# h's rows packed into 120: experts, shared adapter, logits, constant

## The reference, cut to what matters

```
# conditioning of x
q_emb = relu(cond @ W3 + b3)                         # 64 x 512
v     = (64 * x + sum_over_tokens(x)) * q_emb        # per batch
y     = relu(v @ W2 + b2)
# feed-forward with E = 6 routed adapters of rank R = 16, and one shared
base   = y @ W_base + b_base
shared = (y @ A_s) @ B_s
gates  = softmax(y @ W_router + b_router);  w = the two largest gates, 0 elsewhere
h      = y @ A_r[e] for each e;  routed = sum_e (h_e * w_e) @ B_r[e]
out    = x + base + shared + routed
```

## Time and profile before

| | us |
|---|---|
| median of 3 runs (lowest, highest) | 247.85 (246.45, 248.17) |
| the profiled execution | 246.59 |
| its span, first to last instruction | 244.9 |
| TensorE busy in it | 235.0 (96%) |
| DVE, ACT, POOL busy | 177.4, 102.1, 55.7 |

### The profile page before, as it was taken

The page is one execution under the profiler, slowest core; times in us unless marked ns, Lnnn a source line. Parts: engine busy times, 40 slices in busy tenths (PEclk is TensorE's granted clock), DMA queues, the critical chain, the costliest instruction groups (busy, mean ns, idle before and its releaser), DMA issues.

```text
span 244.9 us, 3159 instructions
## 1 busy us (share of the span) xinstructions
PE 235.0 (96%) x1007; PEld 189.4 (77%) x1007; DVE 177.4 (72%) x324; ACT 102.1 (42%) x206; POOL 55.7 (23%) x58
## 2 busy tenths in 40 slices
PE   7699599999999999999999999999999999999994
PEld 2577378888887878888888888888888888888883
DVE  0697898869988996679766995679756995351344
ACT  2247557234434445245533455145433455134330
POOL 5078971202312041012302121012202121000000
PEclk9769979999999999999999999999999999999999
DMA  7989990818016368019610567018000530013004
GB/s 151 299 198 208 270 249 1 170 69 280 0 58 116 146 200 171 0 43 299 143 33 0 183 197 137 0 43 300 0 0 0 192 150 0 0 53 120 3 0 173
DMA packets 32219, 28.49 MB, mean 116 GB/s; under 512 B 6173, under 2 KB 22621, under 8 KB 32206
## 3 DMA queue, kind: packets, MB, share of 16 engines
q1 hardware_dynamic: 32050, 28.33, 42.9%
q10 hardware_dynamic: 156, 0.00, 0.0%
HBM read 19.94 MB, written 8.39 MB: 116 GB/s over the span
## 4 chain that ended last, share of the span: by engine, by line
PE 69%; DVE 16%; SPq 6%; DMA 4%; issue 2%; POOL 1%; ACT 1%; POOLq 0%; DVEq 0%
PE m_ps L661 61%; PE hT L661 7%; DMA x_quart<-in_x_dram 4%; DVE xT L424 4%; DVE out_nat L548 3%; DVE x_sum L438 3%; SPq L217 2%; DVE vsum L429 2%; DVE y_lo L452 2%; SPq L205 1%; POOL x_full L284 1%; DVE x_lo L446 1%; SPq L211 1%; PE hT L748 1%; ACT x_hi L321 1%
## 5 line engine op out<-in xcount | busy, mean ns | idle before, releaser
L284 POOL TENSOR_TENSOR x_full<-x_sum,qT 128x512 f32<-128x512 f32 x31 | 37.9, 1222 | 138.5 <-DVE x_sum L438 138.5
L661 PE MATMUL m_ps<-Wb_lo,y_hi 128*128 128x512 f32 x128 | 50.1, 391 | 0.0
L661 PE MATMUL m_ps<-Wb_hi,y_lo 128*128 128x512 f32 x128 | 50.1, 391 | 0.0
L661 PE MATMUL m_ps<-Wb_hi,y_hi 128*128 128x512 f32 x128 | 50.0, 391 | 0.0
L661 PE MATMUL m_ps<-x_hi,W_hi 128*128 128x512 f32 x112 | 43.8, 391 | 0.2 <-DVE x_lo L446 0.2
L661 PE MATMUL m_ps<-x_lo,W_hi 128*128 128x512 f32 x112 | 43.6, 389 | 0.0
L661 PE MATMUL m_ps<-x_hi,W_lo 128*128 128x512 f32 x112 | 43.6, 389 | 0.0
L329 ACT ACTIVATE y_full<-m_ps,b_sb 128x512 f32<-128x512 f32 x32 | 22.0, 688 | 49.3 <-PE m_ps L661 46.4
L424 DVE STREAM_TRANSPOSE xT<-x_quart 128x512 f32<-128x512 f32 x32 | 34.8, 1088 | 7.6 <-DMA x_quart<-in_x_dram 7.6
L452 DVE TENSOR_TENSOR y_lo<-y_full,y_hi 128x512 fp32r<-128x512 f32 x32 | 25.0, 780 | 12.5 <-ACT y_hi L331 12.5
L446 DVE TENSOR_TENSOR x_lo<-x_full,x_hi 128x512 fp32r<-128x512 f32 x32 | 22.9, 719 | 10.9 <-ACT x_hi L321 10.9
(11 more groups left out here) (82 smaller groups left out, 263.7 us busy)
## 6 DMA issues: line engine op xcount, KB each, us to landing
x_quart<-in_x_dram SPq DMA_DIRECT2D x32, 256.0 KB, 4.8
x_nat<-in_x_dram SPq DMA_DIRECT2D x8, 1024.0 KB, 6.0
out_dram<-out_nat SPq DMA_DIRECT2D x32, 256.0 KB, 2.1
W_f<-in_L_cond_W_dram SPq DMA_DIRECT2D x4, 256.0 KB, 6.3
Wb_f<-in_L_ffn_W_base_dram SPq DMA_DIRECT2D x1, 1024.0 KB, 7.0
W_sb<-in_L_cond_W_dram SPq DMA_DIRECT2D x1, 512.0 KB, 6.0
Wd_f<-in_L_ffn_A_r_dram SPq DMA_DIRECT2D x4, 48.0 KB, 3.1
Wu_f<-in_L_ffn_B_r_dram SPq DMA_DIRECT2D x1, 192.0 KB
```

The source lines that it names most:

```text
L284: nc.gpsimd.tensor_tensor(per_batch(x1_full[:, c, :]), per_batch(x1_sum[:, c, :]), qT[:, c, bass.ds(BG * g, BG)].unsqueeze(2).to_broadcast ...
L661: mm = nc.tensor.matmul(psum, lhsT, rhs, start=start and i == 0, stop=stop and i == len(terms) - 1)
```

## The change

h's rows are laid out anew: the experts in rows 0 to 95, the shared adapter in 96 to 111, the logits in 112 to 117, the constant in row 118, one unused row, and no more: H = 120. Everything with one column or row for each row of h gets 120 of them: Wd (f, hi, lo) and pick have 120 columns, Wu, h_sb, hw (full, hi, lo) 120 rows. h's matmuls and the 0/1 matmul write 120 partitions of hT; `up` contracts over 120. ACT copies rows 96 to 119 (24 rows, not 32) into h_head; as the rest of each 32 is no longer written, POOL clears h_head once with one more memset, and ACT waits for it (head_clear). The DMAs of Wd, Wu and b_router go to the new places. Matmul counts and moving columns stay.

```diff
-    ONE = E
-    SH = 16
-    RO = 32
+    RO = 0
+    SH = RO + E * R
+    LG = SH + R
+    ONE = LG + E
+    H = ONE + 2
+    HEAD = SH
-    assert ONE < SH and SH + R <= RO and RO + E * R == P and TT == KC and NG % 2 == 0 and NG >= 4
+    assert HEAD % S == 0 and H - HEAD <= S and H <= P and TT == KC and NG % 2 == 0 and NG >= 4
...
-        h_sb = sb("h_sb", [P, TG])
+        h_sb = sb("h_sb", [H, TG])
-        gate_logits = h_nat[:, :, 0:E]
-        hw_full = sb("hw_full", [P, TG])
-        hw_hi = sb("hw_hi", [P, TG], F32R)
-        hw_lo = sb("hw_lo", [P, TG], F32R)
+        gate_logits = h_nat[:, :, LG - HEAD:LG - HEAD + E]
+        hw_full = sb("hw_full", [H, TG])
+        hw_hi = sb("hw_hi", [H, TG], F32R)
+        hw_lo = sb("hw_lo", [H, TG], F32R)
-        Wd_f = sb("Wd_f", [P, KC, P])
-        Wu_f = sb("Wu_f", [P, D])
+        Wd_f = sb("Wd_f", [P, KC, H])
+        Wu_f = sb("Wu_f", [H, D])
-        Wd_hi = sb("Wd_hi", [P, KC, P], F32R)
-        Wd_lo = sb("Wd_lo", [P, KC, P], F32R)
-        Wu_hi = sb("Wu_hi", [P, D], F32R)
-        Wu_lo = sb("Wu_lo", [P, D], F32R)
+        Wd_hi = sb("Wd_hi", [P, KC, H], F32R)
+        Wd_lo = sb("Wd_lo", [P, KC, H], F32R)
+        Wu_hi = sb("Wu_hi", [H, D], F32R)
+        Wu_lo = sb("Wu_lo", [H, D], F32R)
...
-        pick_one = sb("pick_one", [S, P])
-        pick = sb("pick", [P, P], F32R)
+        pick_one = sb("pick_one", [S, H])
+        pick = sb("pick", [P, H], F32R)
...
-        idle_ready = sem("idle_ready")
+        idle_ready, head_clear = sem("idle_ready"), sem("head_clear")
...
-            sp.dma_start(Wd_f[:, :, 0:E], W_router.rearrange("(k p) e -> p k e", p=P)).then_inc(Wd_loaded, 16)
+            sp.dma_start(Wd_f[:, :, LG:LG + E], W_router.rearrange("(k p) e -> p k e", p=P)).then_inc(Wd_loaded, 16)
-                sp.dma_start(Wd_f[:, k, RO:P].rearrange("p (e r) -> p e r", r=R),
+                sp.dma_start(Wd_f[:, k, RO:SH].rearrange("p (e r) -> p e r", r=R),
-            sp.dma_start(Wu_f[RO:P, :], B_r.rearrange("e r d -> (e r) d")).then_inc(Wu_loaded, 16)
+            sp.dma_start(Wu_f[RO:SH, :], B_r.rearrange("e r d -> (e r) d")).then_inc(Wu_loaded, 16)
...
+            nc.gpsimd.memset(h_head[:, :], 0.0).then_inc(head_clear, 1)
-            experts = pick_one[:, RO:P].rearrange("p (e r) -> p e r", r=R)
+            experts = pick_one[:, RO:SH].rearrange("p (e r) -> p e r", r=R)
-            nc.gpsimd.affine_select(out=pick_one[:, 0:RO], in_=pick_one[:, 0:RO], compare_op=ALU.not_equal, fill=1.0,
-                                    base=-2 * E, pattern=[[0, RO]], channel_multiplier=1).then_inc(pick_step, 1)
+            nc.gpsimd.affine_select(out=pick_one[:, SH:H], in_=pick_one[:, SH:H], compare_op=ALU.not_equal, fill=1.0,
+                                    base=-2 * E, pattern=[[0, H - SH]], channel_multiplier=1).then_inc(pick_step, 1)
...
-            act.dma_start(h_bias[0:E, :], b_router.rearrange("(e a) -> e a", a=1)).then_inc(bias_loaded, 16)
+            act.dma_start(h_bias[LG:LG + E, :], b_router.rearrange("(e a) -> e a", a=1)).then_inc(bias_loaded, 16)
...
+            act.wait_ge(head_clear, 1)
...
-                    nc.scalar.activation(h_head[q * S:(q + 1) * S, :], hT[0:S, q * P:(q + 1) * P], ACT.Identity,
-                                         bias=h_bias[0:S, 0:1]).then_inc(h_head_ready, 1)
+                    nc.scalar.activation(h_head[q * S:q * S + H - HEAD, :], hT[HEAD:H, q * P:(q + 1) * P], ACT.Identity,
+                                         bias=h_bias[HEAD:H, 0:1]).then_inc(h_head_ready, 1)
-                nc.scalar.activation(h_sb[:, :], hT[:, :], ACT.Identity, bias=h_bias[:, 0:1]).then_inc(h_ready, 1)
+                nc.scalar.activation(h_sb[:, :], hT[0:H, :], ACT.Identity, bias=h_bias[0:H, 0:1]).then_inc(h_ready, 1)
...
-                nc.vector.tensor_tensor(hw_full[:, toks], hT[:, toks], h_sb[:, toks], ALU.mult).then_inc(hw_ready, 1)
+                nc.vector.tensor_tensor(hw_full[:, toks], hT[0:H, toks], h_sb[:, toks], ALU.mult).then_inc(hw_ready, 1)
...
-                product(hT[:, :], [(Wd_hi[:, k, :], y_hi[:, k, :]),
+                product(hT[0:H, :], [(Wd_hi[:, k, :], y_hi[:, k, :]),
-                mm = product(hT[:, :], [(Wd_hi[:, k, :], y_lo[:, k, :])], False, k == KC - 1)
+                mm = product(hT[0:H, :], [(Wd_hi[:, k, :], y_lo[:, k, :])], False, k == KC - 1)
...
-                nc.tensor.matmul(hT[:, :], pick[:, :], w_quads[:, :], start=True, stop=True).then_inc(gates_done, 1)
+                nc.tensor.matmul(hT[0:H, :], pick[:, :], w_quads[:, :], start=True, stop=True).then_inc(gates_done, 1)
```

## The result

The changed kernel takes 250.50 us (median of 6 runs, 250.23 to 252.54) against 247.50 us before (6 runs, 246.45 to 248.17). The ratio is 1.0151, with a 95% interval of 1.0124 to 1.0179. The profiled execution took 251.13 us, with a span of 249.4 us against 244.9.

A forecast was written before the change was run, and what follows sets the result against it. TensorE's distance between matmul starts (0.2267 us) times their count was taken as the bound; -0.1 + 0 + 0 + 0 on the profiled 246.59 us gave 246.5, put at 247.7 as the median, range 246.0 to 252.

The forecast's parts named there:

- a later start: Rival at TensorE's start: A_r's pieces going to odd places delay the quarters by 2 to 4 us; 250 to 252, chance 0.06.
- partly hidden loads: At the 104 matmuls with 120 columns: loads only partly drawn under the stream, time between 248 and 256 us.
- ACT and DVE: h_head, h_sb and the hw tensors keep free sizes, lose partitions: 0 us; Wd_lo saves 0.1 us on POOL, off the path.
- Weights of 120 columns: 104 of 968 float32r matmuls load 120 columns, still stream 512: -0.1 us, at best 1.4 us less.
- 13.3 ns of each distance: In each full-clock TensorE matmul: what the 0.2267 us between starts holds beside the 213.3 ns of its 512 columns.
- The first rival: At the 104 matmuls with 120 columns: loads not hidden under the stream cost 83 ns each, 8.6 us, 256.5; chance 0.16.
- its own sign: In TensorE's chain: h's 9-matmul piece longer than 2.04 us while the 60-matmul piece stays 13.60, load records above 188 ns.
- The second rival: At the 104 matmuls with 120 columns: shorter loads shrink the distance by 12 ns each, 1.2 us, to 246.6; chance 0.12.
- The estimate of 3.8 us: At the 104 matmuls with 120 columns: fast loads lost below 128 columns, 37 ns each, all exposed, 3.8 us more.
- Weights with 120 rows: up's 96 matmuls lose 8 partitions, keep their columns: priced at nothing, far ends 1.3 us gain and 8.0 us loss.
- The memset: POOL's added clearing of h_head: moves the work behind it by up to 0.2 us, covered by 8 us of waiting.
- those zeros: 0 us each for the memset, ACT's added wait and the DMAs to new places (DMA bounds -1 and +5.7 us).

The follow-up runs named there:

- the shifted kernel: The kernel before with only an unused tensor of 1920 bytes per partition ahead of W2_hi, all loads 128 columns: 251.02 us against 246.74, ratio 1.0173.

## Why the prediction was wrong

The forecast was 247.7 us, no change; measured was +1.5%, beyond the 1% that was called no change. That 250.5 us lies in the range given (246 to 252) is luck: the upper part stood there for a later start and for partly hidden loads, and neither made the time.

What bounds the kernel was read rightly: the distance between matmul starts, times their count. The chain after is made of the same pieces, each a little longer.

The step that failed is in "ACT and DVE" and "Weights of 120 columns": the narrower tensors were priced by the instructions that touch them, and by nothing else. A tensor that gets shorter also moves every tensor behind it, and that was in no term of the sum: the distance of 0.2267 us was taken as given for all 968 matmuls because every row had it, whatever was loaded. The runs showed in its place that the distance depends on where the two operands lie; off the multiple of 256 bytes it is 232 ns. That is worth 1.46 to 2.00% when done alone (the shifted kernel), and the changed kernel has it in full. The prediction had the clue in hand. It noted that 13.3 ns of each distance have no explanation at full clock and asked "where these come from"; it tied them only to the count of columns loaded (a guess of 0.8 ns for each narrow load) and not to where the operands lie. It also saw that they are absent at the low clock, and so is the loss by a bad place. What the 13.3 ns are at a place that fits stays open.

The first rival, narrow loads that lose their cover, forecast the right sign and was given 0.16. Its mechanism is wrong in place and form: it allowed for 104 matmuls, 83 ns each, while 968 got some 5 ns each; its own sign, a longer h piece beside an unchanged 60-matmul piece, did not come. What is true of it is small: 1.0 us by the pieces of the chain (the times lost 0.5 to 0.7%, up's 120 rows among it) when the load ends at an unfit place, nothing measurable when it ends at a fit one. The second rival, a shorter distance, was seen nowhere: with 120 columns the load records do get shorter (181 to 182 ns, from 188, between 100 and 240 us) and the starts don't follow.

The estimate of 3.8 us from the Trainium skill's rule on fast loads ("TensorE: Matmul & The Clock Gate", "Weight-path perf modes — Fast Weight Load (FWL) and DoubleRow") lies near the loss measured, by accident; the quarter that it uses is what the section gives as theory for fp8. A kernel without a narrow load lost as much, one with all 104 of them lost nothing, and in the steady stretches the load records of 120 columns are shorter than those of 128. The trace had float32r loads as long as those of the type that the rule excludes, and the runs agree that no fast load was lost.

"Weights with 120 rows" was priced at nothing; it is 0.4 us by the trace, too small for the times (ratio 1.0018, interval 0.9998 to 1.0037). The memset was covered as worked out: POOL was done at 4.3 us and waited 8.80 us then. The layout as a whole, DMAs and ACT's new wait among it, came to a ratio of 1.0011, so those zeros hold. The start moved by 0.4 us in the profile, which the range had room for.

## What to carry to other kernels

Changing one tensor's width moves all the others; before a width change is judged by its time, the same kernel should run with the freed bytes left as a gap. Where matmuls stream back to back, look at the distance of their starts: an even distance means that weights and stream fit, an uneven and longer one in matmuls that nobody touched points at places in memory (or, smaller, at loads of fewer than 128 rows, as in up). Here operands of a matmul should lie a multiple of 256 bytes apart, and a narrow weight tile should be placed by its last column.

## What was not expected of the hardware

- The place of a matmul's two operands against each other in a partition changes the distance of starts from 226.7 ns (differences of 0 or 256 bytes modulo 512) to a mean of 229 to 234 (offsets of 32, 64, 128 and 192 bytes), with float32r, 128 x 128 weights and 512 columns at full clock. At the low clock it changes nothing (426 or 427 ns with gaps of 32, 64 and 1920 bytes). Moving both operands by 128 bytes does not matter (ratio 1.0000); other absolute places were not tried. The Trainium skill's page "TensorE: Matmul & The Clock Gate", in "Step-by-step: what each phase is for", says that loading the next weights doesn't steal read bandwidth from the running matmul, since the two have read ports of their own. Here the distance does depend on the two addresses against each other, by 1 to 3% of a matmul. That this is the two reads getting in each other's way is argued, not seen: no trace shows the reads.
- A narrow load has to fit by its end: 120 columns at 233 ns with the first column in place, 227 with the last.
- The disturbance outlasts its cause by a few matmuls (6 in 1.39 us behind h, where 1.36 is even) and then dies out (the 42 behind take 9.53 us, 9.52 being even).
- What in the memory makes the period 256 bytes, and why 120 rows disturb at a fit place, no run here tells. Nor was it tried whether float32r alone behaves so.
